# Two weight pieces of a decoder layer unpacked later, beside the first gated network

## The reference, cut to what matters

```
q, k, v = x @ wq.T, x @ wk.T, x @ wv.T              # 16 heads of 16
q = (q @ fq1.T + b) * (q @ fq2.T + b);  k likewise
o = causal linear attention(q, k, v), RMS norm per head, times norm_w
x = layernorm(x + o @ wo.T)
kv = x[:, :, None] * ctx[:, None]                   # long convolution with 16 filters
x = layernorm(x + sum(conv(kv, filter) + kv * skip) * ctx)
W = LUT[4-bit code] * scale per block of 32          # gate, up, down: 2048 x 256
x = layernorm(x + (gelu(x @ Wg.T) * (x @ Wu.T)) @ Wd.T)
```

## Time and profile before

| what | us |
|---|---|
| median of 3 runs | 540.75 (540.54 to 542.11) |
| the profiled execution | 540.84 |
| its span, first to last instruction | 539.0 |
| TensorE busy | 521.3 (97%) |
| VectorE busy | 369.4 (69%) |
| ScalarE busy | 153.2 (28%) |
| GpSimd busy | 125.6 (23%) |
| first group's front | about 0 to 103 |
| first network beside the second front | about 103 to 225 |

### The profile page before, as it was taken

How to read it: one execution, slowest core, us unless ns; L and a number is a source line. 1 busy time by engine, 2 the same in 40 slices (tenths; PEclk the granted TensorE clock), 3 DMA queues, 4 the chain that set the end, 5 groups by cost and what they waited for, 6 DMA issues and landing times.

```text
span 539.0 us, 8767 instructions
## 1 busy us (share of the span) xinstructions
PE 521.3 (97%) x3335; PEld 424.2 (79%) x3335; DVE 369.4 (69%) x774; ACT 153.2 (28%) x277; POOL 125.6 (23%) x194
## 2 busy tenths in 40 slices
PE   8999899899999999999999999999999999999994
PEld 8746676667888888867888888866888888888883
DVE  5998989878595678865454768875464777743335
ACT  4564300333422112331333111241332101333230
POOL 3000198210014452220004444120013570100001
PEclk9999999999999999999999999999999999999998
DMA  5662321401111110050001110040001210010001
GB/s 158 170 184 79 88 78 52 136 21 49 51 29 29 52 49 1 0 193 5 1 1 49 50 50 11 1 152 6 1 1 49 69 40 1 2 39 1 1 0 39
DMA packets 25256, 26.80 MB, mean 50 GB/s; under 512 B 2816, under 2 KB 22784, under 8 KB 25216
## 3 DMA queue, kind: packets, MB, share of 16 engines
q1 hardware_dynamic: 14752, 16.26, 9.8%
q10 hardware_dynamic: 10032, 8.43, 5.4%
q0 software_dynamic: 432, 1.57, 0.8%
HBM read 24.15 MB, written 2.10 MB: 49 GB/s over the span
## 4 chain that ended last, share of the span: by engine, by line
PE 84%; DVE 9%; issue 3%; DMA 1%; POOL 1%; ACT 1%; POOLq 0%; DVEq 0%; SPq 0%; ACTq 0%
PE bank L1157 17%; PE bank L1158 16%; PE bank L1159 16%; PE front_bank L1320 5%; PE front_bank L1323 5%; PE front_bank L1321 5%; PE front_bank L1228 3%; PE front_bank L1214 3%; PE front_bank L1157 2%; PE front_bank L1159 2%; PE front_bank L1158 2%; PE front_bank L1290 2%; DMA raw_s<-in_up_s 1%; PE front_bank L1263 1%; DVE st L864 1%
## 5 line engine op out<-in xcount | busy, mean ns | idle before, releaser
L1157 PE MATMUL bank<-x2T_lo,ffn_hi 128*128 128x512 f32 x256 | 109.7, 429 | 1.4 <-DVE x2T_lo L1043 1.4
L1158 PE MATMUL bank<-x2T_hi,ffn_lo 128*128 128x512 f32 x256 | 100.7, 393 | 0.0
L1159 PE MATMUL bank<-x2T_hi,ffn_hi 128*128 128x512 f32 x256 | 100.7, 393 | 0.0
L1099 DVE TENSOR_TENSOR inter<-bank,inter 128x512 f32<-128x512 f32 x63 | 43.5, 691 | 82.6 <-PE bank L1159 82.4
L533 POOL TENSOR_TENSOR qbd<-qT_sb,ctxT_sb 128x256 f32<-128x256 f32 x128 | 79.4, 643 | 67.5 <-PE front_bank L1323 54.0
L474 POOL TENSOR_TENSOR ve<-ve,minus_half 128x2 f32<-128x2 f32 x24 | 18.4, 766 | 306.9 <-DVE ve L869 248.5
L727 ACT ACTIVATE inter_hi<-inter 128x512 fp32r<-128x512 f32 x63 | 39.8, 632 | 145.5 <-DVE inter L1099 145.5
L1157 PE MATMUL bank<-ffn_lo,inter_hi 128*128 128x256 f32 x256 | 76.3, 298 | 1.2 <-DVE inter_lo L1088 0.9
L714 ACT ACTIVATE inter<-bank 128x512 f32<-128x512 f32 x64 | 38.2, 597 | 128.5 <-PE bank L1159 128.5
L1158 PE MATMUL bank<-ffn_hi,inter_lo 128*128 128x256 f32 x256 | 71.6, 280 | 0.0
L1159 PE MATMUL bank<-ffn_hi,inter_hi 128*128 128x256 f32 x256 | 71.1, 278 | 0.0
(11 more groups left out here) (145 smaller groups left out, 775.0 us busy)
## 6 DMA issues: line engine op xcount, KB each, us to landing
toep_sb<-in_toep ACTq DMA_DIRECT2D x64, 128.0 KB, 2.1
xT_sb<-in_xT SPq DMA_DIRECT2D x4, 512.0 KB, 5.5
ctxT_sb<-in_ctxT SPq DMA_DIRECT2D x4, 512.0 KB, 4.8
x_sb<-in_x SPq DMA_DIRECT2D x4, 512.0 KB, 6.0
ctx_sb<-in_ctx SPq DMA_DIRECT2D x4, 512.0 KB, 6.9
out<-ctxT_sb POOLq DMA_DIRECT2D x3, 512.0 KB, 3.4
raw_w<-in_gate_p SPq DMA_DIRECT2D x8, 128.0 KB
raw_s<-in_gate_s SPq DMA_DIRECT2D x8, 128.0 KB
```

Of the source, the lines that this page charges most:

```text
L1099: nc.vector.tensor_tensor(inter[:, n % 2, :], up_ps[:, :], inter[:, n % 2, :], ALU.mult).then_inc(inter_ready, 1)
L1157: nc.tensor.matmul(ps, w_hi, x_lo, start=start, stop=False, skip_group_check=True)
L1158: nc.tensor.matmul(ps, w_lo, x_hi, start=False, stop=False, skip_group_check=True)
L1159: return nc.tensor.matmul(ps, w_hi, x_hi, start=False, stop=stop, skip_group_check=True)
```

## The change

The fourth piece beside the projections is taken out, and so is the piece behind the stage wide. With `BESIDE_PROJ = 3` the score steps begin with piece 4 instead of 5, the first front has 15 pieces instead of 17, and all the pieces left in it come earlier in the list of stages. `SECOND` gets a piece in slot 0, ahead of its up third, and one more in slot 7, ahead of its down third. `FIRST_SCORE` is one less, so TensorE makes the remainders of units 2 to 9 instead of 3 to 10. xT of the second group is loaded at unit 8 instead of 9, its context and rows at unit 17 instead of 19.

```diff
-            return name in ("rms", "wide", "factor", "norm") or name == "score" and k < NU_S
-        SECOND = [(0, 1, 0) if 1 <= s <= 10 and s != 6 else (0, 0, 0) for s in range(NT)]
+            return name in ("rms", "factor", "norm") or name == "score" and k < NU_S
+        SECOND = [(0, 1, 1 if s == 7 else 0) if s <= 10 and s != 6 else (0, 0, 0) for s in range(NT)]
         START = 1
-        FIRST = START + 4 + sum(with_piece(*stage) for slot in slots for stage in slot)
+        BESIDE_PROJ = 3
+        FIRST = START + BESIDE_PROJ + sum(with_piece(*stage) for slot in slots for stage in slot)
         UNITS_FIRST = FIRST + 2
-        FIRST_SCORE = START + 4
+        FIRST_SCORE = START + BESIDE_PROJ
...
-            turn(None, None, 0, lambda pair: beside(1))
+            turn(None, None, 0, lambda pair: beside(pair < BESIDE_PROJ))
...
-                if u == START + 4 + NU_S // 2:
+                if u == FIRST_SCORE + NU_S // 2:
                     load_xT(1)
```

## The result

Over 15 runs each, the changed kernel took 542.5 us in the median (541.19 to 543.41), the kernel before 541.52 (540.53 to 542.11). The ratio is 1.0023, 95% interval 1.0016 to 1.0029: slower by 0.23%, about 1.2 us (the medians themselves lie 0.98 apart). The kernel before came out at 541.52 and not at the 540.75 of the three runs that the forecast started from. The forecast of +0.53 us had the side right, the absolute 541.3 did not reach the measured time, and the step of +1.2 is more than twice the one forecast.

What follows compares the result with a forecast made beforehand. Bound by VectorE's chain before 68 us and by saturated TensorE from 104 to 225 us, the kernel was forecast at 540.75 - 1.81 + 0.95 + 1.39, that is 541.3 us, range 539.8 to 542.6.

Steps and rivals of the forecast that it cites:

- Piece beside the projections: First group's start: without piece 4 the second score mask comes 0.4 us earlier, by TensorE's idle, not the piece's 2.17.
- The DMA wait: Before the fourth score mask: VectorE's 0.47 us wait for scales vanishes, making 0.87 us gained with the start.
- rival (b): Score steps: scales of unit 7 land late and VectorE waits, costing 1.7 us more, 543.0 us in all; chance 0.08.
- the order in the rings: Queue descriptors are served in ring order, so the xT load issued behind the scales can't hold them up.
- Costs in the slots: Second group's front: added pieces aren't hidden and delay TensorE, 0.95 us in slot 0 and 1.39 in slot 7.
- the prediction's sign: Between 103 and 165 us TensorE's waits grow by about 2.35 us, else the slots' part is wrong.
- The exclusion between VectorE and GpSimd: Slot 0: GpSimd waits for the piece's scale, cost stays 0.95 us; were GpSimd first, some 0.2 more.
- The piece behind wide: First group, behind the inverse root: one VectorE piece instead of two lets the factor product start 0.94 us earlier.
- the prediction's own sign: Turn to the second group comes 1.3 to 2.0 us earlier, else the front's part is wrong.
- The range: Whole kernel: 539.8 to 542.6 us, from a single hidden slot to the upper bounds of both slot costs; chance 0.82.
- the gain of the front: First front: 0.87 + 0.94 = 1.81 us saved, bounds 1.2 and 2.0.

Runs made afterwards that it cites:

- after_delay: Changed kernel with four more filler matmuls (0.9 us) at the first score step; 543.86 us, ratio 1.0047 to the kernel before.
- after_fill: Changed kernel with four filler matmuls between the two sums steps of the first group; 542.64 us, ratio 1.0029 to the kernel before.
- after_dense: Changed kernel with one filler matmul behind each of the eight matmul pairs of the sums; 543.3 us, ratio 1.0035 to the kernel before.
- proj_slot0: Kernel before with only the fourth piece beside the projections moved, into slot 0; 540.75 us, ratio 0.9997.
- wide_g7: Kernel before with only the piece behind wide moved, into the first third of slot 7; 540.38 us, ratio 0.9986.
- wide_slot7: Kernel before with only the piece behind wide moved, into the last third of slot 7; 542.7 us, ratio 1.0019.

## Where the prediction was right and which steps failed

- **Piece beside the projections.** Right: the second mask moved by 0.40, and the saving was TensorE's gap and not VectorE's 2.17 us.
- **The DMA wait.** Right: gone, 0.87 in all at the fourth mask. The rival (b), scales that land late behind the context, didn't occur. When they landed isn't shown, so the order in the rings isn't tested.
- **Costs in the slots.** Right: 0.96 in slot 0 (forecast 0.95; the third mask stands 6.54 behind the first and stood 5.58 behind), 1.37 in slot 7 (forecast 1.39). TensorE's idle marks grew by less than the 2.35 of the prediction's sign, 1.95 (0.85 + 0.95 + 0.90 - 0.75), but the steps moved as computed. The exclusion between VectorE and GpSimd did occur, and GpSimd waited, as the prediction chose. VectorE's and GpSimd's timelines of the changed kernel:

```profile
107.45 0.69 DVE L793 SCALAR_TENSOR_TENSOR weight<-code,raw_s 128x512 f32<-128x512 f16 x1
...
107.66 0.95 POOL L481 TENSOR_TENSOR qbd<-qT_sb,half_sel 128x256 f32<-128x256 f32 x1 [7.95 <-PE front_bank L1229]
```

  The scale kept its 0.69 us; GpSimd's step, begun 0.21 behind it, took 0.95 where it took 0.61 without the piece.
- **The piece behind wide.** This is the step that failed. Its 0.94 is there, as 0.93, only in runs whose clock doesn't fall at the sums; in the others the saving is nothing, and against an undisturbed run of the kernel before the factor product even stands 0.42 later (7.90 instead of 7.48). The text took the second group's projections for work that doesn't change; with the clock at half speed the transposes behind them come 1.41 us later, and then TensorE and not VectorE's piece decides when the factor product starts. So the prediction's own sign, a turn 1.3 to 2.0 us earlier, failed in the profiled execution: the first mask of slot 0 stands 86.95 behind `wv_lo` and stood 87.36 behind it, 0.41 earlier.
- **The missing term.** The sum put TensorE's clock at nothing. It was read from one execution, in which the clock was full up to 534 us, and the front text said so of all stretches that mattered. The kernel before fell in 43 of 98 runs and was undisturbed in 47; of the changed kernel's 32 runs 23 had a fall and 3 had none for certain. A fall costs the kernel before 0.43 or 1.36, by its place, and the changed one 1.35 or 1.4. Group against group, the runs without a fall have median spans of 538.8 before and 539.4 after (only 3 runs), those with one 539.8 and 540.7: 0.6 and 0.9 more, where the forecast's 0.53 is the first and 0.53 to 1.46 the second, by the place of the fall. As an estimate: with 0.45 of the runs at 0.9 on average before and 0.8 of them at 1.37 after, the difference is 0.7 us, which with the forecast's 0.53 makes the 1.2 measured. The 0.8 and 0.45 lie between the counts with and without the runs at 0.995; the split between the two places is not known well enough to call this shown. The shift of the start is no likely rival: `wv_lo` starts at 18.14 on average in the nine traces with three pieces beside the projections and at 18.02 in the nine with four.
- **The base.** 540.75 was the median of three runs, two of them near the undisturbed group. It is 541.52 over 15. The absolute forecast was low by this as much as by the missing term.
- **The range.** 542.5 lies inside 539.8 to 542.6, but by luck: the upper end was made of the bounds on the slots' costs and on the gain of the front at full clock, and the two costs came out as computed.

What stays open is why the changed kernel falls more often. Moving the stretch back by 0.9 us (after_delay) and making the sums denser (after_fill, after_dense) both made falls rarer. The first says that the place matters, since only filler ahead of the stretch was added; the second fits the content as a cause, but its fillers also move what stands behind them. One piece alone (proj_slot0, wide_g7, wide_slot7) gave 7, 5 and some 7 falls in 12 runs, against 23 to 29 in 32 of the changed kernel; but these ran on another chip with no run of the changed kernel beside them, and 12 runs are few. Filler in the kernel before didn't help it (5 falls in 7). With two places 17 to 19 us apart, at either of which a run can fall, both removals shift them against each other and against the start; that this decides is argued, not shown.

## What to carry to other kernels

A piece of work taken off a chain saves only up to what is next late, and that includes a slower mode of another engine that one profiled execution doesn't show: look at the granted clock of several executions, and where it falls in some, work out the change for both. When work is moved into a saturated stretch, place it by the idle marks of its engine: the same piece in the same slot cost 1.37 us in the last third and nothing in the first, and with both pieces placed so (and the last ones moved on to slots 10 to 12) a loss of 0.23% became a gain of 0.26%.

## What the runs showed of the hardware

In this kernel, whose TensorE is busy for 97% of the span, the clock fell at two places: in seven of the 18 traces behind 1.8 us of 8-column matmuls, in three behind some 1.5 us of waiting at the convolution. Each fall lasts 3.4 us at 0.50 and comes in some runs only. Matmuls of 512 columns then last 0.63 us and start 0.43 apart, instead of 0.39 and 0.23. Filler that costs 0.9 us between the narrow matmuls made falls rarer in the changed kernel (2 to 5 of 12 runs instead of 23 to 29 of 32) without making it slower in the median (542.64 against 542.5 and 543.06), and 1.8 us of it left one in six runs, at a median of 543.3. A GpSimd product that met a VectorE scale already under way took 0.95 us instead of 0.61.
